# A vision-transformer tower on one core: multiplications that nobody reads, put into TensorE's waits

## The reference, cut to what matters

```python
h = tok(x)                                   # unfold, performer, unfold, performer, unfold, projection
h = concatenate([cls_tok, h], axis=1)        # 32 x 65 x 192
h = h + attention12(layernorm(h))            # 12 heads of 16 values, over the 65 tokens of an image
u = layernorm(h); u = u + attention12(ln1(u))
h = h + u + sum over the top-2 experts e of score[e] * w2[e] @ gelu(w1[e] @ ln2(u))
h = h + ssm(layernorm(h))                    # four small MLPs, then a scan over the 65 tokens, 16 states
u = layernorm(h)
h = h + score[e] * W3[e] @ (silu(W1[e] @ u) * (W2[e] @ u))      # e: the top-1 expert
```

## Time and profile before

| | |
|---|---|
| runs | 1948.37, 1954.43, 1961.23 us; median 1954.43 |
| profiled execution: span (the page gives no other time of it) | 1956.3 us |
| PE busy | 1616.0 us (83%), 11223 instructions |
| DVE, ACT, POOL busy | 1066.6 (55%), 785.8 (40%), 736.8 us (38%) |
| granted clock of TensorE | 10 of 10 where work is dense; 5 to 9 in slices that hold stage ends, routings and narrow multiplications |

### The profile page before, as it was taken

How to read it: one execution, slowest core, us unless ns; L and a number is a source line. 1 busy time by engine, 2 the same in 40 slices (tenths; PEclk the granted TensorE clock), 3 DMA queues, 4 the chain that set the end, 5 groups by cost and what they waited for, 6 DMA issues and landing times. The chain is left out here.

```text
span 1956.3 us, 34891 instructions
## 1 busy us (share of the span) xinstructions
PE 1616.0 (83%) x11223; PEld 1252.7 (64%) x11224; DVE 1066.6 (55%) x3202; ACT 785.8 (40%) x1481; POOL 736.8 (38%) x680
## 2 busy tenths in 40 slices
PE   3889999959999958887987889997299477767897
PEld 2657777747888844775777779996277233356454
DVE  2678988856766533377286511221710599952332
ACT  0457777723555513372264421211245423324211
POOL 2556767622222205142333023432200299930332
PEclk9989999989999968797988779999599799966999
DMA  3244343323434222000000645552600666625331
GB/s 62 43 93 80 76 81 73 75 65 95 112 110 113 56 58 61 2 2 13 1 2 19 177 116 147 160 155 70 138 1 1 169 156 166 153 69 136 109 95 44
DMA packets 222927, 163.90 MB, mean 84 GB/s; under 512 B 117019, under 2 KB 199912, under 8 KB 222302
## 3 DMA queue, kind: packets, MB, share of 16 engines
q1 hardware_dynamic: 209913, 146.94, 29.9%
q0 software_dynamic: 6528, 14.19, 2.7%
q10 hardware_dynamic: 6374, 1.33, 0.4%
HBM read 106.05 MB, written 32.35 MB: 71 GB/s over the span
## 5 line engine op out<-in xcount | busy, mean ns | idle before, releaser
L2156 POOL TENSOR_TENSOR ssm_scan_prod<-ssm_scan_S,ssm_crep 128x1056 f32<-128x1056 f32 x48 | 159.3, 3320 | 147.1 <-DVE ssm_scan_S L2173 147.1
L1279 PE MATMUL a_psum<-a2w_W,a_hT 128*128 128x256 f32 (+1 forms) x640 | 150.8, 383 | 5.4 <-DVE a_z L1071 4.5
L755 PE MATMUL a_psum<-a_W,a_hT 126*128 126x256 f32 x512 | 135.6, 398 | 0.0
L1279 PEld LDWEIGHTS a_psum<-a2w_W,a_hT 128*128 128x128 f32 (+1 forms) x640 | 119.8, 192 | 21.2 <-issue 6.6
L2197 PE MATMUL ssm_scan_psum<-ssm_ST,ssm_EW 112*128 112x512 f32 (+1 forms) x288 | 104.6, 501 | 24.1 <-PEq L1908 20.5
L2747 PE MATMUL moe_tiles_psum<-moe_tiles_XT,moe_tiles_mine 96*128 96x128 f32 x960 | 118.9, 281 | 2.4 <-DMA moe_tiles_mine<-moe_W 2.4
L2747 PEld LDWEIGHTS moe_tiles_psum<-moe_tiles_XT,moe_tiles_mine 96*128 96x128 f32 x960 | 113.2, 195 | 5.4 <-DMA moe_tiles_mine<-moe_W 2.9
L2173 DVE TENSOR_TENSOR_SCAN ssm_scan_S<-ssm_scan_X,ssm_scan_psum 128x1056 f32<-128x1056 f32 x48 | 113.0, 2354 | 4.3
L755 PEld LDWEIGHTS a_psum<-a_W,a_hT 126*128 126x128 f32 x512 | 91.3, 193 | 30.8 <-issue 21.8
L2197 PEld LDWEIGHTS ssm_scan_psum<-ssm_ST,ssm_EW 112*128 112x128 f32 x288 | 51.8, 193 | 91.9 <-issue 68.5
L543 POOL TENSOR_TENSOR a_rstd<-a_rstd,a_mhalf 128x8 f32<-128x8 f32 x64 | 105.1, 1642 | 5.0
(11 more groups left out here) (646 smaller groups left out, 3924.5 us busy)
## 6 DMA issues: line engine op xcount, KB each, us to landing
ssm_scan_grep<-gains SPq DMA_DIRECT2D x48, 528.0 KB, 4.8
moe_tiles_mine<-moe_W SPq DMA_DIRECT2D x40, 576.0 KB
a2w_X<-t SPq DMA_DIRECT2D x192, 96.0 KB
t<-a_O SPq DMA_DIRECT2D x128, 64.0 KB
xrows<-in_x SPq DMA_DIRECT2D x30, 192.0 KB
glu_tiles_mine<-glu_W1r SPq DMA_DIRECT2D x24, 234.5 KB
a_X<-xrows SPq DMA_DIRECT2D x60, 91.9 KB, 3.0
a_PX<-t SPq DMA_DIRECT2D x96, 48.0 KB
```

The lines of the kernel that those rows point to most:

```text
L755: last = nc.tensor.matmul(KQ[q][:, j, :], hT[0:MAIN, q, PARTS * j:PARTS * j + PARTS], W[0:MAIN, :], start=False, stop=True)
L1279: last = nc.tensor.matmul(KQ[:, j, :], hT[i % 2][0:rows, k, PARTS * j:PARTS * j + PARTS], W[0:rows, k, :], start=(k == 0), stop=(k == 4))
L2156: nc.gpsimd.tensor_tensor(prod[n % 2][:], S[n % 2][:], crep[:, cols], ALU.mult).then_inc(s_prod, 1)
```

## The change

A helper `turn_over` issues n multiplications of the identity by itself, spread to 512 columns, into one PSUM bank that holds nothing read later. It is called at the start of most stages, in waits at their ends, and between narrow multiplications. In `moe`'s routing `nbanks` goes from 5 to 4 and the banks are numbered through all experts, which leaves bank 7 to the helper. Some calls stand behind new waits, and the stage that sums the slots gets a TensorE function of its own.

```diff
+def turn_over(nc, ps, bank, ident, n):
+    to = ps[:, bank * BANK:(bank + 1) * BANK].rearrange("p (a b) -> p a b", a=4)
+    for _ in range(n):
+        nc.tensor.matmul(to, ident[:], spread(ident[:], 1, 4), start=True, stop=True)
 # tokens
+            pe.wait_ge(s["stat"], 2)
+            turn_over(nc, ps, 7, ident, 3)
             for t in range(steps + 6):
...
+                if steps + 2 <= t < steps + 5:
+                    turn_over(nc, ps, 2, ident, 2)
+            for i in range(2):
+                pe.wait_ge(s["po"], steps - 1 + i)
+                turn_over(nc, ps, 2, ident, 2)
+            for q in range(3, PIECES):
+                pe.wait_ge(s[f"rows{q}"], 16)
+                turn_over(nc, ps, 2, ident, 2)
 # attention, prep
                 pe.wait_ge(norm.ident_done, 2)
+                turn_over(nc, ps, 0, ident, 4)
 # attention, images
                         for i in range(IMAGES):
+                            if i % 8 == 4:
+                                turn_over(nc, ps, 5, ident, 1)
...
+                    if t >= PAIRS + 2:
+                        turn_over(nc, ps, 0, ident, 2)
 # ssm, MLPs
                 pe.wait_ge(norm.ident_done, 2)
-                norm.turn(pe)
+                turn_over(nc, ps, 7, ident, 2)
+                pe.wait_ge(norm.root, 1)
+                turn_over(nc, ps, 7, ident, 1)
+                norm.turn(pe, lambda g: turn_over(nc, ps, 7, ident, 1))
...
                 layer2(groups - 1)
+                for kb in range(2):
+                    pe.wait_ge(s_gain, kb + 1)
+                    turn_over(nc, ps, 7, ident, 3)
 # ssm, end of the scan; start of last
+                turn_over(nc, ps, 0, ident, 4)
+                turn_over(nc, ps, 7, ident, 1)
 # experts, routing
-            nbanks = njobs // 2
+            nbanks = 4
                 def body(e):
+                    turn_over(nc, ps, 7, ident, 1)
-                        b = (3 + n % nbanks) * BANK
+                        b = (3 + (njobs * e + n) % nbanks) * BANK
                 pe.wait_ge(norm.ident_done, 2)
+                turn_over(nc, ps, 7, ident, 3)
                 def logits(g):
+                    turn_over(nc, ps, 7, ident, 1)
                 for k in range(slots):
+                    turn_over(nc, ps, 7, ident, 1)
                     pe.wait_ge(s_slot, k + 1)
                     for i in range(NTILE):
+                        if i % 10 == 5:
+                            turn_over(nc, ps, 7, ident, 1)
...
                 for e in (6, 7):
                     body(e)
+                turn_over(nc, ps, 7, ident, 1)
 # experts, tiles
+                turn_over(nc, ps, 7 if direct else 2, ident, 3)
                 schedule(pe, body_direct if direct else body_turned)
 # experts, sum of the slots
+            @block.tensor
+            def _(pe):
+                for q in range(3, PIECES):
+                    pe.wait_ge(s_ga[1][q], 16)
+                    turn_over(nc, ps, 0, ident, 2)
```

More of the change, by code:

```diff
@@ L2882, in experts @@
             s_v = s2.sem("v")
+            ps = s2.psum()
             block = ctx2.enter_context(nc.Block())
+            @block.tensor
[3 more added lines that the diff above has]
+                    turn_over(nc, ps, 0, ident, 2)
             @block.sync
```

## The result

20 runs of each kernel: 1960.27 us median (1951.58 to 1967.20) against 1953.71 (1948.37 to 1963.07). The ratio over all runs is 1.0023, with a 95% interval of 1.0013 to 1.0034 (the medians alone give 1.0034): a little slower, where 1945 was forecast.

The account below looks back on a forecast made before the run. TensorE was taken as busiest in most slices, with joined stages rather than one chain and half clock at five kinds of place. The eleven parts summed to -8.9 us: 1947.4 profiled, 1945 in the median's terms, range 1922 to 1964.

Parts of the forecast that it names:

- part 4: Attentions' key loops, line 1704: four calls in line each time keep it warm; -2.5 us (-4.6 to +17.8).
- rival B: Calls between narrow multiplications (key loops, logits, slots) don't hold the clock; some 25 us more, 1979 us; chance 0.10.
- Price of a call: One added 512-column multiplication, two instructions, takes 0.9 us at full clock and 1.9 us at half clock.
- Parts 1 and 2: `tokens`: warm start -2 us (-3 to 0); its end, where the last calls wait for rows, +1 (-1.6 to +4).
- Part 3: Preparation of the attentions, four calls each: -2 us (-2.8 to +1), with nothing taken in `fa`.
- Part 5: End of images stages and `last`, four calls each: `last` starts warm; -3 us for both (-5.3 to +4).
- Parts 6 and 10: First and second routing, calls among logits and slot multiplications: -0.2 us (-4 to +27) and -0.1 (-3 to +18).
- Part 8: `ssm` MLPs, eight calls before and in the transpositions, delay hidden by loads: -0.8 us (-2 to +1.5).
- Part 9: Scan's end, four calls in idle time, and start of `ssm` `last`, one in line: +2.2 us (0 to +5).
- Part 11: First tile of `glu`, three calls in a wait, first instructions warm: -1.5 us (-1.5 to +1).
- Part 7: Tiles of `moe` and sum of the slots: 0, first tile waits for DMAs, sum's calls on an otherwise idle engine.
- Rival D: Transpositions don't hold the clock, so gains in attention preparation and routings fall away: 1952 instead of 1945 us; chance 0.05.

Follow-up runs that it names:

- experiment 7: The changed kernel with 8 instead of 4 calls in each key loop; 1956.40 us, run once.
- experiment 9: The changed kernel with each key loop's four calls in one group ahead of the loop; 1959.25 us, run once.
- 10: The changed kernel with calls only at starts of tokens, attentions, ssm MLPs, last experts' tiles, and ends of images stages; 1944.57 us, ratio 0.9951 to before.
- 12: The kernel of 10 with the second pair's scores issued inside the key loop; 1942.28 us, ratio 0.9947 to before.
- 11: The kernel of experiment 1 with the second pair's scores issued inside the key loop, order alone; 1947.73 us, ratio 0.9960 to before.
- experiment 4: The kernel of experiment 1 without the calls behind the last two steps of the images stages; 1952.94 us, ratio 0.9982 to before.
- 5: The kernel of experiment 1 with calls behind only the last step of the images stages, not the last two; 1950.58 us, ratio 0.9977 to before.
- 3: The kernel of experiment 1 also without the calls among both routings' narrow multiplications (logits, slots); 1948.96 us, ratio 0.9965 to before.
- experiment 6: The kernel before with the first routing's four banks instead of five and no added calls; 1955.16 us, ratio 1.0002 to before.
- experiment 1: The changed kernel without its calls in the two key loops; 1946.34 us, ratio 0.9963 to the kernel before.

## Why the prediction was wrong

The time lies inside the stated range, but on the other side of before than the forecast. The step that failed is **part 4**, line 1704. It worked out the sequence "all warm", 128 x 59 ns + 4 x 0.9 = 11.1 us, and so took for granted that four calls hold the clock. They don't: 18.8 and 18.6 us, +7.4 and +5.3 where -0.3 and -2.2 stood. That is 15.3 us between the forecast and the loop, more than the 11.9 between the forecast's -8.9 and the profiled +3.0. The upper end of the part (21.3 us each) was right as a mechanism. I kept it for rival B only, and B was priced as all four sequences or half of them falling together. What happened lies between: in the key loops the clock fell, in the logits and slots it didn't. The argument against B was wrong, too: one call among 32 narrow instructions is not enough, one among 16 is (experiment 7), and four calls ahead of the loop are not (experiment 9).

Even by its own sum the part was a poor bet, which could be seen without a run. Where the calls hold the clock they still stand in line, 3.6 us of them, and the sum gave -0.3 in `at` for it and -2.2 in `fa`: 2.5 us to win. What was lost when the clock fell was 12.8, five times as much. The lower end, -4.6 with the first pairs of images warm, isn't borne out either: experiment 7 held the clock and the rest of the stage was no shorter.

The other steps by their own terms:

- *Price of a call*: 0.9 and 1.9 us forecast; 0.92 to 0.95 and 1.85 measured. Right.
- *Parts 1 and 2*, -1 together: -0.4. The start gives about 3 us by experiments 10 and 12 (`tokens` 301.1 and 301.4 against 304.4), the far end of its range, and the end costs 2 to 4.5, by the same two against the profiles that have it (303.4 to 305.6), where +1 was forecast: 2.1 of it stands behind the last rows, because its calls run at half clock. Nothing was won at the end.
- *Part 3*: `at` -2.4 for -2 here, but nothing in the profiles of 9 and 11 with the same calls. `fa` -1.3 for 0: small, and in the range; in 4 and 5, which have these calls but not both pairs behind the images stages, it is 74.5 as before, so these calls alone did not give it.
- *Part 5*: -5.0 in the `last` stages and, with the loops taken out, +0.8 and +1.2 in the images stages; -3.0 in all, as forecast (experiment 4 agrees, and adds some 2 us in `fa`).
- *Parts 6 and 10*: -0.2 and -0.6 for -0.2 and -0.1. The clock held in the logits and slots of both and the calls cost what it gave; the times of experiments 3 and 10 say the same from the other side, though their single routings differ by more (81.1 and 78.5 in `moe`, 71.1 and 67.3 in `glu`). The banks cost nothing (experiment 6).
- *Part 8*: -2.5 for -0.8. Line 2053's first 88 instructions take 19.66 us for 22.71, and most of the 3.05 is kept: ScalarE's table load hid less of it than I took. In the profile of 11 they take 21.28, and the stage 143.7 as before. *Part 9*: +0.5 for +2.2: the calls at the scan's end fit the wait before the join (5.17 us, done 0.3 before the next stage), and the one in `last` costs 0.7. *Part 11*: -0.7 for -1.5; in the other profiles with these calls the stage lasts 145.4 to 148.7 us, 146.5 before, so that a gain is not shown.
- *Part 7*, 0: the tiles of `moe` were 1.6 us longer; in the other profiles with the same calls they were 228.2 to 232.1 us, so this can't be told from nothing.
- *Rival D*: against it stands the first routing of the changed kernel, TensorE:

```profile
1075.71 1.47 PE L2457 MATMUL moe_route_psum<-moe_ident,moe_raw_first 128*96 128x128 f32 x12
1077.02 1.82 PE L2461 MATMUL moe_route_psum<-moe_ident,moe_raw_second 96*128 96x96 f32 x12
1078.68 0.88 PE L1872 MATMUL moe_route_psum<-moe_ident,moe_route_xn 104*96 104x104 f32 x8
1080.06 1.15 PE L1872 MATMUL moe_route_psum<-moe_ident,moe_route_xn 104*96 104x104 f32 x8 [0.50 <-ACT moe_route_xT L1893]
```

  Forty transpositions with no call between them, 5.3 us to the next one, and the clock is 1.00 throughout; the narrow multiplications of the key loop had lost it after 4.0 us at the latest. By what the Trainium skill ("TensorE: Matmul & The Clock Gate", Part 4) says of transpose-mode work the full clock would not have engaged there, so this trace does not agree. The fall in 9 and 11 came behind transpositions, but behind idle time too, and the runs don't separate the two.

The forecast's sum without part 4 is -6.4; measured without the two loops it is 3.0 - 12.8 = -9.8, and experiment 1, which is that kernel, came out 8.6 us below before by the medians. What stays open is why the first routing differs by up to 4 us between profiles of the same code, why the second attention's key loop keeps the full clock longer where both pairs stand behind the images stages, and whether 5 to 7 calls would hold a key loop.

## What to carry to other kernels

A multiplication that nobody reads pays only in time in which TensorE would be idle, ahead of work that starts at half clock and that its stage waits for: here the starts of stages. Even there it must reach up to that work: calls that were done before it, with idle time behind, bought nothing in two profiles. In line among narrow multiplications it has a price of its own, and if there are too few it is paid twice over while the clock falls anyway, so work out first what an all-warm sequence would save, and whether the smallest number of calls that holds the clock costs less than that. And before a stage's join, whatever stands last on TensorE is part of the stage.

## What the runs showed of the hardware

- Narrow multiplications (6 columns, 128 in a row, TensorE busy throughout) lost the full clock 1.0 to 4.0 us after they began, in both loops of every profile with none or four calls among them. When in that span it fell differed between profiles of the same loop, and was worth 2 us (11.06 and 13.26).
- One 512-column pair for every 32 of them didn't hold the clock (0.50 for 15.8 us); one for every 16 did (1.00 for 15 us, twice).
- Four such pairs just ahead of the loop didn't carry it: it fell 3.5 us into the narrow work.
- At the end of `tokens` six such pairs ran at full clock; after 3.1 us of idle time the next two took 3.23 us where 2.0 are full speed, so half clock came back while they ran. At the end of the images stage of 5 two pairs took 3.60 us behind 1.3 us of idle time and 24 instructions; in 1, without that idle time, 1.98.
- Forty float32 transpositions in 5.3 us, 0.5 of them idle, with no other work between them, kept the full clock (1.00).
